# Limits on node counts by degree in steps of 32 instead of 128, in a graph kernel that gathers features slot by slot

## The reference

```python
def layer0(feat, efeat, W_msg, b_msg, W_attn, b_attn, src, dst):
    w_m = (efeat @ W_msg + b_msg).reshape(E, 16, 16)
    w_a = (efeat @ W_attn + b_attn).reshape(E, 16, 16)
    h = feat[src][:, :, None]
    e1, e2 = w_m * h, w_a * h
    ex = exp(e2 - segment_max(e2, dst)[dst])
    attn = ex / segment_sum(ex, dst)[dst]
    return segment_sum(e1 * attn, dst).sum(axis=1)

def layer1(edge_attr, dst):
    return segment_sum(edge_attr, dst) / max(count(dst), 1)

x = layernorm(x + layer0(...))
x = layernorm(x + layer1(edge_attr, dst))
```

## Time and profile before

| | us |
|---|---|
| median of 3 runs | 2221.29 (2220.6 to 2221.82) |
| the profiled execution, its own time | 2220.79 |
| its span, from the first to the last instruction | 2218.9 |
| PE busy | 1965.3 (89%) |
| DVE busy | 1819.1 (82%) |
| POOL busy | 1662.2 (75%) |
| ACT busy | 1252.1 (56%) |
| granted TensorE clock, mean | 0.959 of full speed |

### The profile page before, as it was taken

How to read it: one execution, slowest core, us unless ns; L and a number is a source line. 1 busy time by engine, 2 the same in 40 slices (tenths; PEclk the granted TensorE clock), 3 DMA queues, 4 the chain that set the end, 5 groups by cost and what they waited for, 6 DMA issues and landing times.

```text
span 2218.9 us, 21991 instructions
## 1 busy us (share of the span) xinstructions
PE 1965.3 (89%) x6682; PEld 892.4 (40%) x6682; DVE 1819.1 (82%) x3094; ACT 1252.1 (56%) x1228; POOL 1662.2 (75%) x1791
## 2 busy tenths in 40 slices
PE   1697989978989899999999999998889998899995
PEld 0433434433444444444444444443434443344442
DVE  7787878876887888889888889878778888899984
ACT  4355646555555556566656566655555555466552
POOL 6777777777777777777777777777777777777776
PEclk9788999989999999999999999999999999999998
DMA  6201000000000001000000010000010000101000
GB/s 237 87 14 19 16 13 13 9 17 13 13 13 13 13 13 18 13 13 13 17 12 12 12 17 12 12 17 12 12 17 12 16 12 16 33 15 22 10 7 5
DMA packets 60074, 47.61 MB, mean 21 GB/s; under 512 B 28366, under 2 KB 55439, under 8 KB 59436
## 3 DMA queue, kind: packets, MB, share of 16 engines
q0 software_dynamic: 57632, 29.73, 8.5%
q1 hardware_dynamic: 2316, 16.40, 2.0%
HBM read 44.01 MB, written 1.90 MB: 21 GB/s over the span
## 4 chain that ended last, share of the span: by engine, by line
PE 44%; POOL 23%; DVE 18%; issue 11%; ACT 2%; DMA 1%; POOLq 0%; DVEq 0%; SPq 0%; ACTq 0%
PE PX L1136 33%; POOL AR L658 20%; PE PW L1116 8%; DVE AR L1486 8%; DVE AR L1499 3%; PE PTB L1105 2%; DVE AR L1518 2%; ACT PX L947 1%; POOL y_d L701 1%; DVE AR L1304 1%; POOL CS L709 1%; POOL out L759 1%; DVE AR L1520 0%; DVE AR L1511 0%; POOL AR L663 0%
## 5 line engine op out<-in xcount | busy, mean ns | idle before, releaser
L658 POOL DMA_INDIRECT AR<-in_xt,AR x1607 | 1526.2, 950 | 493.2 <-issue 478.8
L1136 PE MATMUL PX<-AR,CS 128*128 128x512 f32 x3246 | 1553.6, 603 | 7.3 <-ACT AR L901 6.2
L1486 DVE CUSTOM_DVE_ANT_1 AR<-PW,AR 128x1024 f32<-128x1024 f32 x815 | 970.5, 1220 | 256.4 <-PE PW L1116 99.3
L1136 PEld LDWEIGHTS PX<-AR,CS 128*128 128x128 f32 x3246 | 606.1, 193 | 522.5 <-issue 424.9
L1116 PE MATMUL PW<-WS,LT 100*128 100x512 bf16 x1630 | 511.7, 397 | 161.0 <-DVE AR L1486 157.7
L1499 DVE TENSOR_TENSOR AR<-AR,PX 128x1024 f32<-128x1024 f32 (+1 forms) x442 | 500.3, 1132 | 71.6 <-ACT PX L947 46.7
L953 ACT ACTIVATE PX<-AR 128x1024 f32<-128x1024 f32 (+1 forms) x221 | 212.4, 961 | 485.2 <-DVE AR L1499 483.7
L949 ACT ACTIVATE AR<-AR 128x2048 f32<-128x2048 f32 (+1 forms) x221 | 413.0, 1869 | 7.2
L1116 PEld LDWEIGHTS PW<-WS,LT 100*128 100x128 bf16 x1630 | 150.6, 99 | 654.1 <-issue 399.6
L947 ACT ACTIVATE PX<-AR 128x1024 f32<-128x1024 f32 (+1 forms) x221 | 231.5, 1047 | 119.0 <-DVE AR L1499 117.5
L895 ACT ACTIVATE LT<-PTB 100x1024 bf16<-100x1024 bf16 (+1 forms) x221 | 208.8, 945 | 127.3 <-PE PTB L1105 127.1
(11 more groups left out here) (194 smaller groups left out, 451.9 us busy)
## 6 DMA issues: line engine op xcount, KB each, us to landing
AR<-in_xt,AR POOLq DMA_INDIRECT x1607, 2.3
AR<-in_eat SPq DMA_DIRECT2D x3, 3128.0 KB, 12.1
AR<-in_eat SPq DMA_DIRECT2D x1, 3120.0 KB, 12.1
y_d<-AR SPq DMA_DIRECT2D x1, 784.0 KB, 13.7
AR<-y_d SPq DMA_DIRECT2D x1, 784.0 KB, 4.7
AR<-in_es,E0I POOLq DMA_INDIRECT x48, 3.4
y_d<-AR POOLq DMA_INDIRECT x36, 2.1
CS<-in_cst SPq DMA_DIRECT2D x1, 455.0 KB, 5.4
```

Of the source, the lines that this page charges most:

```text
L658: g.indirect_dma_start(feat(h, j - j0, j - j0 + 1), None, xt, bass.IndirectOffsetOnAxis(ap=node, axis=0)).then_inc(hg_sem(h), 16)
L1136: i = pe.matmul(PDR, IDN, x, start=(a == 0 and j == 0), stop=(g == LAST[k] and j == n - 1))
L1486: v.tensor_tensor_reduce(em(g, j, j + 2).rearrange("p (x c) -> p x c", c=32), w, hb, 1.0, LOW, ALU.mult, ALU.max, accum_out=MXC[:, k % 2, ...
```

## The change

The table of upper limits is no longer 128 times the number of tiles whose cap reaches a degree. It is written out as LIMIT, in multiples of 32. The caps are derived from it: a tile's cap is the largest degree that more than 128 x rank nodes may reach. This makes three caps smaller by one (ranks 32, 38 and 47, which get 29, 27 and 21 slots) and leaves all tiles' rounded sizes DEG as they are; the lower limits RLOWS of two tiles become smaller by one with their caps. HELD gives the number of partitions that slot j of tile k needs at most. It is below 128 for 31 of the 1604 slots (7 times 32, 9 times 64, 15 times 96), and `gather` uses it for the number of rows. The host writes LIMIT into the place of CAPB.

```diff
-RCAPS = [56, 45, 43, 41, 40, 40, 39, 38, 38, 37, 37, 36, 36, 35, 35, 35, 34, 34, 34, 33, 33, 33, 32, 32, 32, 32, 31, 31, 31,
-         30, 30, 30, 30, 29, 29, 29, 28, 28, 28, 27, 27, 26, 26, 25, 25, 24, 23, 22]
+LOB, HB = 21, 26
+LIMIT = [6080, 6016, 5952, 5824, 5664, 5440, 5184, 4864, 4512, 4096, 3680, 3264, 2784,
+         2368, 1984, 1632, 1312, 1056, 864, 672, 512, 384, 288, 192, 160, 96]
+RCAPS = [56] + [max(d for d in range(LOB, LOB + HB) if LIMIT[d - LOB] > 128 * r) for r in range(1, NC - 1)]
...
-LOB, HB = 21, 26
...
+def HELD(k, j):
+    d = min(j + 1, LOB + HB - 1)
+    return 128 if k == 0 or d < LOB else min(128, LIMIT[d - LOB] - 128 * RANKS[k - 1])
...
-                    node = SRC0[:, j:j + 1] if k == 0 else XE[:, at:at + 1]
-                    g.indirect_dma_start(feat(h, j - j0, j - j0 + 1), None, xt,
+                    p = HELD(k, j)
+                    node = SRC0[:, j:j + 1] if k == 0 else XE[0:p, at:at + 1]
+                    g.indirect_dma_start(feat(h, j - j0, j - j0 + 1)[0:p, :], None, xt,
                                          bass.IndirectOffsetOnAxis(ap=node, axis=0)).then_inc(hg_sem(h), 16)
...
-    cst[:, 820:884] = [128 * sum(c >= d for c in RCAPS) for d in range(BINS)]
+    cst[:, 820 + LOB:820 + LOB + HB] = LIMIT
```

## The result

The kernel takes 3587.23 us (3586.65 to 3587.9, four runs) where before takes 2220.94 (2220.02 to 2221.82, four runs): a ratio of 1.6153, 95% interval 1.6129 to 1.6177. The profiled execution took 3587.69 us with a span of 3585.8.

What follows compares the result with a forecast made beforehand. POOL, full with 1607 gathers, bounds the kernel before, but the guard would send the changed one to general(): 402 + 3585 (239 tiles of 15.0) + 175 = 4162, and 2 around the span, about 4165 us; range 3650 to 4850.

Steps and rivals of the forecast that it cites:

- the fallback: general(), the path all five engines take when the guard fails; priced at about 4165 us, 1.88 times before.
- The guard: Test at line 1420: 6144 nodes stand in the lowest bin or above, over its new limit 6080, so general() runs.
- Until the loop starts: general() before its tile loop: search, block reads, gathers, scatters, small HBM round trips; 402 us, bounds 360 and 450.
- After the loop: general() after its tiles: last stores, join over tile borders, seven gather groups, layer norms, output; 175 us, bounds 140 and 220.
- A tile: One of 239 turns of general()'s loop: 15.0 us, 3585 us in all.
- the ring: In general()'s loop: row maximum, PE's transposes and first messages, ACT's 32 products, last messages, DVE's tree; 13.3 us at full clock.
- half clock: PE at half its granted clock in general()'s loop: 15.6 us a tile, taken two times in three.
- The small product: ACT's 32 products of 32 elements a tile in general(): 0.21 us each with overlap, 6.7 us; 0.31 without.
- Rival 2: general() slower: ACT's products don't overlap or PSUM reads cost more; 18.8 us a tile, 5072 us; 0.20 including above 4520.
- Rival 3: general() bound by POOL: PE keeps its clock, DVE's 12.9 us is the period; 3662 us; 0.16 including below 3925.
- Rival 1: The guard passes, the regular path runs with fewer and partial gathers: 2217.6 to 2204.8 us, middle 2211; chance 0.06.

Runs made afterwards that it cites:

- f_bin0: The changed kernel with only the lowest bin's limit put back to 6144; 2216.14 us, ratio 0.9982.
- g_bin0: The kernel before with only the lowest bin's limit lowered from 6144 to 6080; 3584.23 us, ratio 1.6146.
- p_thin: The changed kernel with six of PE's eight sum matmuls per tile left out; 3834.66 us, ratio 1.7265.
- d_gm2: The changed kernel with DVE's two products by the exponentials cut from 1024 to 32 elements each; 3568.27 us, ratio 1.6066.
- both_seven: The changed kernel, DVE's two exponentials' products cut to 32 elements, ACT's 32 products made 16 of 64, one of eight sum pairs left out; 3406.05 us.

## Why the prediction was right about the guard and wrong about the price of the fallback

**The guard: right.** The reading of the clip and of SUF, from 6144 > 6080 to TOT, is what `f_bin0` and `g_bin0` show.

**Until the loop starts: 402 forecast, 378 measured.** The search is done at 181.9 us (193): the 42 block reads that wait for DVE start 1.24 us apart where 1.42 was priced, and one of its 50 steps takes 0.62 us and not 0.75. POOL's first gather starts at 189.5, where about 206 was allowed, for the source indices were there 4.6 us after the clearing; the last scatter starts at 315.7, where the forecast had it landed at 350. From there to the first product it is 63 us, where 52 and some 3 for the landing were allowed.

**After the loop: 175 forecast, 201 measured** by the same division. The groups of seven gathers went as priced (three DVE steps of 1792 at 2.03 us and one at 3.15). What was short is the part ahead of them: the first gather starts at 3437.5 us, 52 us behind the last tile's turn, where 28 was allowed for the last sums and the join.

**A tile: 15.0 forecast, 12.58 measured. This is where it failed,** in two steps of about equal size, and in the size of the ring under them.

*"PE's work is 6.2 us of a tile at full clock", and "the ring leaves PE idle for some 4 us in each tile, so I take half clock two times in three".* PE's busy share of 0.855 is 10.8 us of a tile. The eight sum matmuls were priced at 0.434 each; but the group of L1216 counts 3824, and 3824 / 239 = 16 a tile. One fp32 matmul call of 512 columns leaves two records here, 0.434 us each. The kernel before had said so: its L1136 has 3246 records for the 1623 matmuls that the groups of slots add up to, and the 13.90 us by 32 of the earlier trace rows are 16 matmuls. With 8 x 0.43 = 3.5 us more PE's work is 9.7 us; the other 1.1 lie in the small matmuls and transposes and were not split up. PE's idle time is 1.8 us a tile and not 4, in pieces of 0.87 us at most in the turn shown, and the clock is 1.00. (By its own figures the forecast left PE idle for 13.8 - 6.2 = 7.6 us at full clock; its 4 does not follow from them.) The forecast's own two prices were 13.8 at full clock and 15.6 at half; the step from 13.8 to 15.0 is 1.2 x 239 = 287 us. The price of the half clock with all sums in was not tested: `p_thin`, at 0.69, has 13.65 us a tile, but without most of them.

*"DVE: sum 12.9, with waits for semaphores 13.8".* From 1500.56 to 1513.03 DVE's rows give 12.47: maximum tree 2.33 for 2.44, the two products in SBUF 2.25 for 2.6, small ones 0.79 with the 0.24 of waiting in it, the scans and the five products with PSUM as priced. 0.9 us of waits were added, and 0.24 are there: DVE runs behind PE and finds nearly every semaphore already up. 13.8 - 12.58 = 1.22, times 239 is 292 us. That and the clock are the 578.

*The ring at full clock, 13.3 us.* It would have been the bound in the forecast once DVE came below it, so it was too long as well. The largest part of that is ACT: 7.4 us for the 32 products and the copy of the sums, where the timeline after has 6.41 (from 1502.57 to 1508.98).

**ACT.** The small product was taken at 0.21 us with overlap; 16 stand in 2.97 us, 0.186 each. By ScalarE: Activation LUTs of the Trainium skill the estimate was 214 ns, closer than no overlap (0.31) and still 15% high. Rival 2 fell on this and on the clock.

**The rivals.** Rival 3 (PE keeps its clock, DVE 12.9: 3662) came nearest. Its conditions on the clock and on DVE's semaphores held, the one on ACT's products did not (0.186 and not 0.13), and POOL, after which it was named, sets nothing. Its floor of 3280 counted POOL's 11.3 us for all 239 tiles, though the last 52 have one DMA each. It was given 0.16, and with 12.5 for DVE, as its rows have it, it would have said 577 + 2988 + 2 = 3567. The forecast's own sentence, that a period under 14 means ACT or the clock was priced too high, applies for both. Rival 1's other side was measured by `f_bin0`: 2216.14, inside 2204.8 to 2217.6. The lean to 2211, its middle, was wrong: the gather's time goes only a tenth by rows.

**The ring as drawn is there, behind DVE.** `p_thin` runs on it step by step. In `d_gm2` PE's eight transposes and four sums take the place of DVE's product and tree in it, 12.5 us, a branch that the forecast had kept for half clock. In the kernel after it is hidden by DVE's 12.5, by so little that each covers the other. What the forecast did not have is a third path: `both_seven` shows a ring of 11.7 us with four of the eight sums and ACT's copy of them inside, and ACT's products beside it.

**A version that beats both.** `f_bin0`, 2216.14 us against 2220.28: the limit of the lowest bin has to stay at 128 x 48, because every node outside tile 0 is clipped into that bin or above. 0.2% is all that the finer limits give.

## What to carry to other kernels

A table that feeds a guard has entries that hold by counting alone (all nodes are at or above the lowest bin): check each against what the kernel counts before asking what a tighter table saves. Before saying that PE idles, price its work by records per call (the count in the groups over the calls in the code); an fp32 matmul here is two. And when taking one cost away moves nothing, take two away together before calling either of them free.

## What the runs showed of the hardware

- An indirect gather of 64-byte rows costs POOL 0.947 us for 128 rows and 0.863 for 32, and 0.30 us to the next in both cases: rows are nearly free, instructions are not.
- Small activations of 32 elements from PSUM, with a scale from a tile, run at 0.186 us from start to start in a run of 16, while one record alone shows a mean of 363 ns. The mean of a group is no price for a pipelined run.
- PE kept the granted clock at 0.99 to 1.00 from 400 to 3380 us with 10.8 of 12.6 us busy and, in the turn shown, idle pieces under 0.9 us; with a piece of 3.2 to 3.3 us in each of `p_thin`'s four tiles after 1500 us the mean was 0.69, and taking away PE's work cost 247 us.
- After a load of an activation table the next activation starts 1.29 us after the load did, with nothing between the two (ACT's timeline of the kernel after):

```profile
3450.72 1.28 ACT L1052 ACT_TABLE_LOAD   x1
3452.01 1.70 ACT L1052 ACTIVATE AR<-AR 128x1792 f32<-128x1792 f32 x1
```
